# Expert weights loaded by SyncE at a row number held in a register, in place of GpSimd's gather

## The chip, the cores and the metric

The kernel runs on one core of a Trainium2 chip. The metric is the device time of one execution in microseconds (us). TensorE is PE in the rows (its weight loads PEld), VectorE is DVE, ScalarE ACT, GpSimd POOL and SyncE SP; a name with a q behind it (SPq) is that engine's instruction queue, where transfers are issued.

## What is computed

The block takes x of 4 x 2048 tokens with 256 features. It normalises each token, runs attention of 16 heads with a distance bias over it, and multiplies the result by a gate that comes from a mixture of experts (8 experts with 128 hidden features, two chosen for a token, and a shared one). The experts are what the change touches.

```python
xn = layernorm(x)
s = attention(xn)                       # 4 batches x 16 heads, 2048 keys, bias -slope*|i-j|
topk_idx = top_k(masked, 2)[1]          # two experts of 8 for a token
comb = (one_hot(topk_idx, 8) * topk_w[..., None]).sum(1)
g = einsum('th,ehi->tei', xn, w_gate)
u = einsum('th,ehi->tei', xn, w_up)
y = einsum('tei,eih->teh', silu(g) * u, w_down)
routed = einsum('teh,te->th', y, comb)
shared = silu(xn @ sw_gate) * (xn @ sw_up) @ sw_down
return x + s * silu(routed + shared)
```

## The kernel before

The program has three stages that follow one another. `tokens_stage` normalises, projects to queries, keys and values, and writes packed expert weights to a scratch tensor `w_rows` in DRAM: 8 experts x 128 rows, each row 768 floats (gate and up weights of one input row as pairs of half-precision numbers, then the row of the down weights). `attend_stage` does the attention and, spread through it, the routing and the experts. `deliver_stage` projects the heads' results, multiplies by the gate and stores.

In `attend_stage` the scores of all 64 heads (4 batches x 16) are cut into 1306 chunks of at most 1024 columns. Every engine runs the same list of chunks in its own written order: PE computes the scores of chunk c+3 (`scores`, L1385), ACT takes the exponential of chunk c (L1502), DVE multiplies the diagonal pieces (`fade`, L1527), and PE multiplies the probabilities with the values (`weighted_sum`, L1411). The heads alternate between wide ones (up to 32 chunks) and narrow ones (down to 8).

The experts' work is hung into this list. Routing sorts all token choices by expert into 72 tiles of 256 slots. `owner` (128 x 72 whole numbers, written by DVE in L1714) holds, for tile i and partition p, the row of `w_rows` that partition p needs: 128 times the tile's expert, plus p. `row_of` holds the tokens of a tile, `back_of` the places for its results. Once DVE has written these (`order_ready`, L1576, at chunk 209 in head 10), tile i goes through these steps, each fixed to a chunk by the table `FF_AT`, one tile for each 11300 columns (`FF_EACH`): PE turns the token rows (`turn_tile`, L1441), DVE takes them (L1550, L1552), PE multiplies with gate and up weights (`gate_up`, L1451, after a wait for `w_in`), ACT and DVE form the hidden features (L1493, L1583, L1586), PE multiplies with the down weights (`down`, L1457, which raises `ff_down`), DVE copies the result (L1593).

The weights of three tiles have room at a time (`w[:, i % 3, :]`), the token rows (`xs`) and results (`ys`) of two. GpSimd does all the traffic by indirect transfers, in a written order with waits for a chunk number (`expd`), the pace: for tile i two stores of the results of tile i-1 (`store_rows`, L1334), two gathers of the token rows of tile i+2 (`load_rows`, L1328), one gather of the weights of tile i+2 (`load_weights`, L1322). The pace numbers are columns behind the turn of a tile: stores at 500 and 5100, token rows at 2800 and 7400, weights at 9700.

SyncE runs a loop over the 64 heads n. In it, in this order: it waits until the result of head n-1 has been read out (`out_ready`) and stores it (`store_head`, L987 and L988); in some heads it loads the sums of a batch; it loads the raw values of head n+2 (`load_v`, L1079); it waits until all scores of head n are done (`scored`) and loads keys and queries of head n+3 (`load_head`, L1071, four transfers of 256 KB). DVE turns the keys of head n+3 (`turn_k`, L1514) in the middle of head n+2.

Of the kernel before, what the change touches and what calls it, by code (L numbers as in the profile page):

```python
# [19 lines left out]
P = 128  # L20
# [21 lines left out]
SLOTS = 3  # L42
# [13 lines left out]
MIX_FROM, MIX_TO = 364, 397  # L56
PAIRS_AHEAD = 2
PADDING = P
PACE_YS, PACE_XS, PACE_W = (500, 5100), (2800, 7400), 9700
BIAS = 1 + 3 * HD  # L60
STEEP = 3
XS = 2.0 ** 11
# [1003 lines left out]
def load_head(engine, keep, n):  # L1066
    par = n % STACKS
    for dst, stack in ((keep["K"][par], keep["k_stack"]), (keep["Q"][par], keep["q_stack"])):
        rows = stack[row_of_head(n) * HALF:(row_of_head(n) + 1) * HALF, :]
        for half in range(2):  # L1070
            engine.dma_start(dst[HALF * half:HALF * (half + 1), :], rows).then_inc(keep["stacks_in"][par], 16)  # L1071


def load_v(engine, keep, n):
    par = n % 2
    b, h = divmod(row_of_head(n), H)
    v_rows = keep["values"].rearrange("(j p q) k -> j p (q k)", p=P, q=TT)
    src = v_rows[b * BPB:(b + 1) * BPB, :, h * TT * HD:(h + 1) * TT * HD].rearrange("g p k -> p g k")
    engine.dma_start(keep["V_raw"][par][:].rearrange("p (g t) d -> p g (t d)", g=BPB), src).then_inc(keep["v_loaded"][par], 16)  # L1079


def attend_stage(nc, a, keep):
# [54 lines left out]
    with ExitStack() as ctx:  # L1137
# [106 lines left out]
        with nc.Block() as block:  # L1244
            @block.sync
            def _(sp):
                def load_sums(b):
                    for par in range(2):
                        sp.wait_ge(o_out[par], STORED * (H // 2) * (b + 1))
                    if b > 0:  # L1250
                        sp.wait_ge(inverted, 6 * b)
                        sp.wait_ge(proved, 9 * b)
                    sp.dma_start(sums[:], keep["sums"][(b + 1) * H:(b + 2) * H, :].rearrange("h (e c) -> (h e) c", c=D)).then_inc(sums_in, 16)
                    load_shifts(sp, keep, b, sums_in)

                def store_recips(b):
                    sp.wait_ge(inverted, 6 * (b + 1))
                    store_inverse(sp, keep, b, recip_out)

                load_head(sp, keep, 2)  # L1260
                for dst, src in route_loads:
                    sp.dma_start(dst, src).then_inc(route_loaded, 16)

                sp.dma_start(keep["stats"], keep["stat"][0:3 * VW].rearrange("p j t -> p (j t)")).then_inc(peaks_out, 16)

                def load_pair():
                    sp.wait_ge(peaks_out, 16)
                    sp.wait_ge(routed, 1)
                    for b in range(B):
                        sp.dma_start(q_peaks[:, b], keep["stats"][0:H, b * KT:(b + 1) * KT].rearrange("h (e t) -> h e t", t=2)).then_inc(peaks_in, 16)  # L1270
                    sp.dma_start(keep["limit"][:], a["limit"]).then_inc(peaks_in, 16)
                    sp.dma_start(k_peaks.rearrange("p b k -> p (b k)"),
                                 keep["stats"][VW:VW + H, :].unsqueeze(1).broadcast_to([H, P // H, B * KT])).then_inc(peaks_in, 16)

                for n in range(BH):
                    b, h = divmod(n, H)
                    if n >= 1:
                        sp.wait_ge(out_ready, n)
                        store_head(sp, keep, n - 1, o_out)
                    if b > 0 and h == 2:  # L1280
                        load_sums(b - 1)
                    if b > 0 and h == SIDE_FROM + 1:
                        store_recips(b - 1)
                    if n + STACKS == H:
                        sp.wait_ge(const_in, 48 * (B - 1))
                    if n == H + 1:
                        load_pair()
                    if n + 2 < BH:

                        sp.wait_ge(v_in, n + 1)  # L1290
                        load_v(sp, keep, n + 2)
                    if n + STACKS < BH:
                        sp.wait_ge(scored, FIRST_CHUNK[n + 1])
                        load_head(sp, keep, n + STACKS)
                    if b == 0 and 3 <= h < 3 + 3 * (B - 1):
                        store_constant(sp, a, keep, (h - 3) // 3 + 1, (h - 3) % 3, const_in)
                sp.wait_ge(recip_out, 48 * (B - 1))
                sp.wait_ge(scored, FIRST_CHUNK[BH - 1])
                for n in range(2):
                    sp.dma_start(keep["inverse"][0:3 * H, n, :], keep["turned"][3 * H * n:3 * H * (n + 1), :]).then_inc(keep["inverse_in"][n], 16)  # L1300
                sp.dma_start(keep["spread"][:].bitcast(U16).rearrange("k c p -> k (c p)"), a["spread"]).then_inc(keep["w_o_in"], 16)
                sp.dma_start(keep["w_o"][:], a["wT_out"].rearrange("(c p) n -> p c n", p=P)).then_inc(keep["w_o_in"], 16)
                sp.dma_start(keep["b_o"], a["b_out"].rearrange("(o n) -> o n", o=1).broadcast_to([P, D])).then_inc(keep["w_o_in"], 16)
                with nc.allow_non_contiguous_dma(reason="256 biases, once"):
                    sp.dma_start(keep["b_v"], a["b_qkv"].rearrange("(c p) -> p c", p=P)[:, 2 * DC:3 * DC]).then_inc(keep["w_o_in"], 16)
                sp.wait_ge(mixed, NT)
                for u in range(BPB):
                    load_block(sp, a, keep, u, keep["o"][:, u], keep["x"][:, u], keep["block_in"][u])

                sp.wait_ge(o_out[0], STORED * (BH // 2))  # L1310
                sp.wait_ge(o_out[1], STORED * (BH // 2 - 1))

            @block.gpsimd
            def _(pool):
                index = lambda ap: bass.IndirectOffsetOnAxis(ap=ap, axis=0)

                def load_weights(i):
                    if i > 2:
                        pool.wait_ge(ff_down, i - 2)
                    if i > 1:  # L1320
                        pool.wait_ge(expd, after("turn", i - 2, PACE_W))
                    nc.gpsimd.indirect_dma_start(w[:, i % 3, :], None, keep["w_rows"], index(keep["owner"][:, i:i + 1])).then_inc(w_in[i % 3], 16)  # L1322

                def load_rows(i, t):
                    if i > 1:
                        pool.wait_ge(ff_turned, i - 1)
                        pool.wait_ge(expd, after("turn", i - 2, PACE_XS[t]))
                    nc.gpsimd.indirect_dma_start(xs[:, i % 2, t, :], None, keep["xn"], index(row_of[:, t, i:i + 1])).then_inc(xs_in[i % 2], 16)  # L1328

                def store_rows(i, t):  # L1330
                    pool.wait_ge(ff_y, i + 1)
                    if i + 1 < TILES_IN:
                        pool.wait_ge(expd, after("turn", i + 1, PACE_YS[t]))
                    nc.gpsimd.indirect_dma_start(keep["ys"], index(back_of[:, t, i:i + 1]), ys[:, i % 2, t, :], None).then_inc(ys_out[i % 2], 16)  # L1334

                def fetch(j):

                    if j >= PAIRS_AHEAD:
                        pool.wait_ge(mixed, TT * (j - PAIRS_AHEAD + 1))
                    for n in range(2):  # L1340
                        pool.wait_ge(expd, fetch_at(j, n))
                        pool.dma_start(pairs[:, j % PAIRS_AHEAD, n], returned[n, j]).then_inc(mix_in[j % PAIRS_AHEAD], 16)

                pool.wait_ge(routed, 1)
                pool.wait_ge(order_ready, 1)
                for i in range(2):
                    load_weights(i)
                    for t in range(2):
                        load_rows(i, t)
                for i in range(TILES_IN):  # L1350
                    for t in range(2):
                        if i > 0:
                            store_rows(i - 1, t)
                        if i + 2 < TILES_IN:
                            load_rows(i + 2, t)
                    if i + 2 < TILES_IN:
                        load_weights(i + 2)
                for t in range(2):
                    store_rows(TILES_IN - 1, t)
                for n in range(2):  # L1360
                    pool.wait_ge(ys_out[n], 32 * (TILES_IN // 2))
                for j in range(NBLK):
                    fetch(j)
# [1837 lines left out]
```

## Time and profile before

| what | value |
|---|---|
| median of three runs | 1667.21 us |
| lowest and highest of them | 1664.34 and 1673.85 us |
| the profiled execution, its own time | 1676.03 us |
| its span, first to last instruction | 1674.1 us |
| mean granted TensorE clock in it | 0.976 |
| PE busy over the span | 1524.8 us (91%) |
| ACT busy | 1318.0 us (79%) |
| DVE busy | 1010.6 us (60%) |
| POOL busy | 496.4 us (30%) |

The busy shares are means over three unlike stages. `attend_stage` lies from about 277 to 1580 us of the span, and the experts' tiles in it from about 484 to 1455 us. The profile's chain of work that ended last reaches back only to about 1581 us, into `deliver_stage`, so it says nothing of the stretch that the change touches; that stretch is read from its windows, its waits and its order of time.

### The profile page before, as it was taken

The page shows a single profiled execution, that of the slowest core. Times are in us where ns is not written, and L with a number is a line of the kernel's source. Part 1 is how long each engine was busy: PE and PEld are TensorE (multiplying, and loading weights), DVE is VectorE, ACT ScalarE, POOL GpSimd, SP SyncE. Part 2 cuts the span into 40 slices and gives each one's busy share as a digit, 9 for nine tenths or more (in the row PEclk, how much of TensorE's full clock was granted, in tenths as well). Part 3 has the DMA queues.
Part 4 walks back from the last instruction along what each step waited for, and adds up shares of the span by engine and source line. Part 5 has one row for each costly group of instructions (what it writes and reads, how often), then busy time and mean ns, then how long its engine had stood idle before and what let it go on. Part 6 is the DMA issues. An engine that isn't in the chain of part 4 may idle for free. (4 is left out here: it accounts for less than half of the span.)

```text
span 1674.1 us, 39958 instructions
## 1 busy us (share of the span) xinstructions
PE 1524.8 (91%) x15328; PEld 680.6 (41%) x15328; DVE 1010.6 (60%) x2738; ACT 1318.0 (79%) x1694; POOL 496.4 (30%) x477
## 2 busy tenths in 40 slices
PE   5898997899989999998999899989999899988996
PEld 3554564223334443343444333434443333322464
DVE  7787765988854454545445444454455444577776
ACT  5788776888888887887888788878888788788721
POOL 1222331000023343343343343434333333222053
PEclk9999998999999999999999999999999999999999
DMA  6858776233345455454444455544545554577795
GB/s 202 274 193 253 259 228 183 68 112 90 90 143 132 131 138 141 138 137 128 137 134 134 126 139 137 140 132 134 131 134 143 135 134 134 132 203 221 244 313 173
DMA packets 201089, 265.58 MB, mean 159 GB/s; under 512 B 90960, under 2 KB 158592, under 8 KB 200640
## 3 DMA queue, kind: packets, MB, share of 16 engines
q1 hardware_dynamic: 168256, 171.72, 36.8%
q0 software_dynamic: 24192, 82.86, 16.1%
q10 hardware_dynamic: 8448, 8.39, 1.4%
q8 instruction: 125, 2.05, 0.5%
q14 instruction: 68, 0.56, 0.1%
HBM read 180.56 MB, written 90.46 MB: 162 GB/s over the span
## 5 line engine op out<-in xcount | busy, mean ns | idle before, releaser
L1502 ACT ACTIVATE probs_att<-SC_att 128x1024 f32<-128x1024 f32 (+10 forms) x1306 | 1075.2, 911 | 181.5 <-PE SC_att L1385 160.4
L1411 PE MATMUL O_att<-probs_att,V_att 128*32 128x512 f32 (+7 forms) x8144 | 642.5, 412 | 50.3 <-DVE probs_att L1527 28.4
L1527 DVE TENSOR_TENSOR probs_att<-probs_att,decay 128x128 f32<-128x128 f32 x1024 | 264.3, 286 | 272.6 <-ACT probs_att L1502 245.9
L1411 PEld LDWEIGHTS O_att<-probs_att,V_att 128*32 128x32 f32 x8144 | 178.4, 111 | 208.7 <-issue 129.4
L1385 PE MATMUL SC_att<-Q,K_turned_att 64*128 64x512 f16 (+7 forms) x1244 | 221.6, 310 | 13.9 <-issue 5.6
L1334 POOL DMA_INDIRECT ys<-ys_att,back_of_att x144 | 144.7, 1005 | 252.9 <-ACT probs_att L1502 226.8
L1328 POOL DMA_INDIRECT x<-xn,row_of_att x144 | 142.8, 992 | 243.2 <-ACT probs_att L1502 226.3
L1385 PE MATMUL SC_att<-Q,K 64*128 64x512 f16 (+9 forms) x1154 | 201.2, 301 | 7.6 <-DVE K_turned_att L1514 7.0
L1385 PEld LDWEIGHTS SC_att<-Q,K_turned_att 64*128 64x128 f16 x1244 | 67.2, 94 | 265.2 <-ACT probs_att L1502 156.7
L1322 POOL DMA_INDIRECT x<-w_rows,owner x72 | 71.9, 999 | 333.6 <-DVE row_of_att L1576 217.3
L699 POOL TENSOR_TENSOR inverse<-qk_tok,inverse 128x512 f16<-128x512 f32 x64 | 75.6, 1189 | 171.4 <-ACT inverse L731 164.3
L1451 PE MATMUL F_att<-x 128*128 128x256 f16 x864 | 111.6, 281 | 1.5 <-issue 1.3
L1385 PE MATMUL SC_att<-inverse,K_turned_att 64*128 64x512 f16 (+7 forms) x602 | 106.3, 309 | 6.2 <-issue 4.5
L1533 DVE COPY out<-O_att 128x512 f32<-128x512 f32 x64 | 44.2, 691 | 105.5 <-PE O_att L1411 89.6
L599 PE MATMUL GU_tok<-xT_tok,w_qkv_tok 128*128 128x512 f16 x384 | 90.9, 388 | 15.5 <-DVE xT_tok L916 15.4
L1385 PEld LDWEIGHTS SC_att<-Q,K 64*128 64x128 f16 (+1 forms) x1154 | 65.4, 95 | 96.8 <-ACT probs_att L1502 46.9
L1457 PE MATMUL F_att<-x 128*128 128x256 f32 x288 | 82.9, 411 | 18.3 <-DVE x L1586 16.3
L1385 PE MATMUL SC_att<-inverse 64*128 64x512 f16 (+8 forms) x560 | 96.7, 299 | 0.4 <-ACT probs_att L1502 0.4
L1593 DVE COPY ys_att<-F_att 128x512 f32<-128x512 f32 x72 | 49.8, 691 | 77.6 <-PE F_att L1457 71.8
L1451 PEld LDWEIGHTS F_att<-x 128*128 128x128 f16 x864 | 80.9, 100 | 26.8 <-issue 15.9
L1550 DVE TENSOR_SCALAR x<-F_att 128x512 f16<-128x512 f32 x72 | 49.7, 690 | 61.5 <-PE F_att L1441 48.2
L1385 PEld LDWEIGHTS SC_att<-inverse,K_turned_att 64*128 64x128 f16 x602 | 32.6, 94 | 122.8 <-ACT probs_att L1502 65.5
(212 smaller groups left out, 1672.4 us busy)
## 6 DMA issues: line engine op xcount, KB each, us to landing
K<-k_stack SPq DMA_DIRECT2D x86, 256.0 KB
Q<-q_stack SPq DMA_DIRECT2D x86, 256.0 KB
x<-ys POOLq DMA_DIRECT2D x32, 512.0 KB, 4.8
x<-in_x SPq DMA_DIRECT2D x24, 512.0 KB, 6.7
k_stack<-inverse SPq DMA_DIRECT2D x96, 128.0 KB
q_stack<-inverse SPq DMA_DIRECT2D x96, 128.0 KB
inverse<-k_stack SPq DMA_DIRECT2D x42, 256.0 KB
inverse<-q_stack SPq DMA_DIRECT2D x42, 256.0 KB
```

Source lines behind the costliest of these rows:

```text
L599: mm = pe.matmul(GU[:, m, :], w_qkv[:, w, c, m * P:(m + 1) * P], xT[:, j % 2, x, c, :], start=(k == 0), stop=(k == len(PRODUCTS) - 1))
L699: nc.gpsimd.tensor_tensor(parts[:, k, 1, :], qk[:, m, :], parts[:, k, 0, :], ALU.subtract).then_inc(part2, 1)
L1322: nc.gpsimd.indirect_dma_start(w[:, i % 3, :], None, keep["w_rows"], index(keep["owner"][:, i:i + 1])).then_inc(w_in[i % 3], 16)
L1328: nc.gpsimd.indirect_dma_start(xs[:, i % 2, t, :], None, keep["xn"], index(row_of[:, t, i:i + 1])).then_inc(xs_in[i % 2], 16)
L1334: nc.gpsimd.indirect_dma_start(keep["ys"], index(back_of[:, t, i:i + 1]), ys[:, i % 2, t, :], None).then_inc(ys_out[i % 2], 16)
L1385: mm = pe.matmul(SC[:, c % SLOTS, at:at + x1 - x0], (K_turned[at_turned] if side else K[at_k])[rows, k * P:(k + 1) * P], Q[at_k][rows, x0: ...
L1411: mm = pe.matmul(O[VW * g:VW * (g + 1), col:col + width * len(mine)], V[par][:, k, :], spans[:, j0:j0 + BPB * (len(mine) - 1) + 1:BPB, :], ...
L1451: mm = pe.matmul(F[:, n * TILE_IN:(n + 1) * TILE_IN], w_of(i, wp, c, n), xT[:, xp, c, :], start=(k == 0), stop=(k == len(PRODUCTS) - 1))
L1457: mm = pe.matmul(F[:, t * D:(t + 1) * D], hid[:, t * P:(t + 1) * P], w[:, i % 3, WGU:WROW], start=True, stop=True)
L1502: nc.scalar.activation(probs[home][:, side + chunk.base:side + chunk.base + chunk.width], SC[:, c % SLOTS, start:start + chunk.width], ACT ...
L1527: v.tensor_tensor(diag, diag, decay[:, head_of(chunk.head), :], ALU.mult).then_inc(faded, 1)
L1593: v.tensor_copy(ys[:, i % 2].rearrange("p t d -> p (t d)"), F[:]).then_inc(ff_y, 1)
```

## The change

`load_weights` moves from GpSimd's program to SyncE's. There it waits for the buffer (`ff_down`), reads the first row number of the tile from `owner` into a register (`value_load`), and issues one plain transfer of 128 rows of `w_rows` from that row on. The first three tiles' weights are loaded in the loop's round for head 11, behind `load_v`; those of a later tile i in the round of the head in which tile i-3 is done with its down product, also behind `load_v` and ahead of the wait and the loads of `load_head`. GpSimd's five transfers of a tile become four, and their pace numbers change: stores at 500 and 6100, token rows at 3300 and 8900.

```diff
-PACE_YS, PACE_XS, PACE_W = (500, 5100), (2800, 7400), 9700
+PACE_YS, PACE_XS = (500, 6100), (3300, 8900)
@@ block.sync
+                def load_weights(i):
+                    if i > 2:
+                        sp.wait_ge(ff_down, i - 2)
+                    first = sp.value_load(keep["owner"][0:1, i:i + 1], min_val=0, max_val=(E - 1) * P)
+                    sp.dma_start(w[:, i % 3, :], keep["w_rows"][bass.ds(first, P), :]).then_inc(w_in[i % 3], 16)
+
@@ loop over the heads, behind load_v
+                    if n == CHUNKS[ORDER_AT].head + 1:
+                        sp.wait_ge(routed, 1)
+                        sp.wait_ge(order_ready, 1)
+                        for i in range(3):
+                            load_weights(i)
+                    for i in range(3, TILES_IN):
+                        if n == max(CHUNKS[ORDER_AT].head + 1, CHUNKS[FF_AT[i - 3]["down"] + SLOTS].head):
+                            load_weights(i)
                     if n + STACKS < BH:
                         sp.wait_ge(scored, FIRST_CHUNK[n + 1])
                         load_head(sp, keep, n + STACKS)
@@ block.gpsimd
-                def load_weights(i):
-                    if i > 2:
-                        pool.wait_ge(ff_down, i - 2)
-                    if i > 1:
-                        pool.wait_ge(expd, after("turn", i - 2, PACE_W))
-                    nc.gpsimd.indirect_dma_start(w[:, i % 3, :], None, keep["w_rows"], index(keep["owner"][:, i:i + 1])).then_inc(w_in[i % 3], 16)
-
                 for i in range(2):
-                    load_weights(i)
                     for t in range(2):
                         load_rows(i, t)
...
-                    if i + 2 < TILES_IN:
-                        load_weights(i + 2)
```

## Rows read from the trace of the kernel before

**Rows 1.** The page's first part: busy time of each engine, share, instructions.

```profile
PE 1524.8 (91%) x15328; PEld 680.6 (41%) x15328; DVE 1010.6 (60%) x2738; ACT 1318.0 (79%) x1694; POOL 496.4 (30%) x477
```

**Rows 2.** Windows: the order's stretch, then all tiles; busy us, clock, DMA share.

```profile
core 0: us, PE busy (x) PEld busy (x) DVE busy (x) ACT busy (x) POOL busy (x), PEclk, DMA share, GB/s
480.00:500.00 20.00, 15.21 (x193) 6.64 (x184) 7.93 (x30) 14.17 (x19) 8.08 (x6) 0.83 0.70 218
500.00:1450.00 950.00, 900.30 (x9811) 380.15 (x9814) 467.19 (x1275) 795.88 (x1001) 348.39 (x351) 0.98 0.50 134
```

**Rows 3.** Groups by line, 500 to 1450 us: busy, mean ns, idle before, releasers.

```profile
L1411 PE MATMUL O_att<-probs_att,V_att 128*32 128x64 f32 (+7 forms) x5832 | 452.2, 408 | 22.3 <-DVE probs_att L1527 9.7 <-DVE out L1533 7.6 <-issue 4.5
...
L1451 PE MATMUL F_att<-x 128*128 128x256 f16 x864 | 111.6, 281 | 1.5 <-issue 1.3
L1457 PE MATMUL F_att<-x 128*128 128x256 f32 x284 | 81.7, 411 | 17.9 <-DVE x L1586 16.3 <-issue 1.5
...
L1322 POOL DMA_INDIRECT x<-w_rows,owner x70 | 67.6, 966 | 116.0 <-ACT probs_att L1502 81.1 <-PE F_att L1457 29.1 <-issue 5.8
```

**Rows 4.** The tile `w_rows`: GpSimd's gather, ns min/median/max, and us to landing.

```profile
L1322 POOL DMA_INDIRECT x<-w_rows,owner x72: 945/947/3332, 484.1 to 1424.0; - x72
...
DMA to landing us min/median/max: 3.0/3.8/5.9
```

**Rows 5.** SyncE in order of time, head 11: start us, us.

```profile
490.48 2.52 SPq L987 DMA_DIRECT2D weighted<-out  x4
...
493.64 0.45 SPq L1079 DMA_DIRECT2D V_raw<-values  x1
```

**Rows 6.** Line 3168, the program's one register load from on-chip memory: ns on SyncE.

```profile
L3168 SPq TENSOR_LOAD <-redo x1: 493/493/493, 1669.7 to 1669.7; - x1
...
L3168 SPq FUSED_REGOPS  x1: 192/192/192, 1670.3 to 1670.3; - x1
L3168 SPq SEQ_ASSERT  x1: 37/37/37, 1670.5 to 1670.5; - x1
```

**Rows 7.** Line 1071, the loads of a head's keys and queries: ns of an issue.

```profile
L1071 SPq DMA_DIRECT2D K<-k_stack x86: 465/594/1845, 125.1 to 1526.1; - x86
```

**Rows 8.** PE in order of time, then line 1451's own row: products with tiles' weights.

```profile
503.06 1.49 PE L1451 MATMUL F_att<-x 128*128 128x256 f16 x12
...
L1451 PE MATMUL F_att<-x x864: 269/273/421, 503.1 to 1448.1; 128*128 128x256 f16 x173
```

**Rows 9.** The tile `x` (the experts' buffers lie in it): us to landing, all transfers.

```profile
DMA to landing us min/median/max: 3.8/5.4/11.7
```

**Rows 10.** SyncE's and PE's order of time around tile 45, the shortest lead.

```profile
1073.61 0.44 SPq L1079 DMA_DIRECT2D V_raw<-values  x1
...
1097.35 1.48 PE L1451 MATMUL F_att<-x 128*128 128x256 f16 x12
```

**Rows 11.** SyncE's own waits over the whole span: us in total, times, longest.

```profile
SPq L1071 <- PE SC_att L1385: 667.9, 46, 26.2
SPq L987 <- DVE out L1533: 197.0, 61, 16.9
```

**Rows 12.** SyncE's and DVE's order of time for head 18: keys loaded, keys turned.

```profile
596.43 1.13 SPq L1071 DMA_DIRECT2D K<-k_stack  x2
...
619.99 0.75 DVE L1514 TENSOR_SCALAR K_turned_att<-K,turn 128x2048 f16<-128x2048 f16 x1
```

**Rows 13.** GpSimd's and PE's order of time for tile 63: rows gathered, rows turned.

```profile
1323.26 0.97 POOL L1328 DMA_INDIRECT x<-xn,row_of_att  x1 [6.95 <-ACT probs_att L1502]
...
1337.04 0.66 PE L1441 MATMUL F_att<-ident,x 128*128 128x128 f32 x4
```

**Rows 14.** Line 1514 on DVE, 500 to 1450 us: ns min/median/max of the keys' turns.

```profile
L1514 DVE TENSOR_SCALAR K_turned_att<-K,turn x31: 743/748/919, 501.9 to 1438.8; 128x2048 f16<-128x2048 f16 x31
L1514 DVE TENSOR_SCALAR K_turned_att<-inverse,turn x15: 744/748/960, 546.6 to 1412.1; 128x2048 f16<-128x2048 f16 x15
```

**Rows 15.** The same line in the groups by line: busy us, mean ns.

```profile
L1514 DVE TENSOR_SCALAR K_turned_att<-K,turn 128x2048 f16<-128x2048 f16 x31 | 23.4, 756 | 0.0
L1514 DVE TENSOR_SCALAR K_turned_att<-inverse,turn 128x2048 f16<-128x2048 f16 x15 | 11.8, 789 | 0.0
```

## The prediction

> **What bounds the kernel now.** I read the page's busy shares first, then windows of the stretch in which the experts' tiles run, then the groups by line in that stretch, and last the order of time around a few tiles. The shares put PE first with 91% of the span and POOL last with 30% [rows 1]. The chain that ended last lies in the final stage, so the stage of the change is read from its windows. From 500 to 1450 us PE is busy 900.3 of 950 us, ACT 795.9, DVE 467.2 and POOL 348.4 [rows 2]. PE is the bound there, and all that any change of waiting can give back is the 49.7 us in which it is idle. The groups by line say who ends that idle time: 22.3 us ahead of the value products, ended by DVE, and 17.9 us ahead of the down products, ended by DVE's hidden features [rows 3]. The products with gate and up weights, the first to need a tile's weights, stood idle 1.5 us in all for 864 matmuls, and no transfer is named [rows 3]. So the weights' arrival doesn't hold PE today. What the reader is to see: GpSimd's gather of the weights has 67.6 us of busy time, but 116.0 us of idle time ahead of it, ended by ACT and PE, which is the written pace [rows 3]. POOL waits for the others; nobody waits for POOL.
>
> **The change part by part.** *GpSimd's 72 gathers go.* 72 x 0.947 us = 68 us less for an engine that is idle 950 - 348.4 = 602 us of the stretch [rows 2, 4]. Worth nothing on PE's path; the cover is POOL's own idle time.
>
> *The bytes stay.* Each load moves 128 rows of 3072 bytes as before, on the same DMA engines, whose mean share is 0.50 [rows 2].
>
> *SyncE gets 72 loads.* The trace has no such load, so its issue is bounded. The one register load that SyncE does, at the program's end, takes 0.493 us, with 0.192 us of register work and 0.037 us of a bounds test [rows 6]; the issue of a 256 KB transfer takes 0.465 to 1.845 us, median 0.594 [rows 7]. Together 1.3 us; the address worked out from the register is not shown, one more 0.192 at the least. I take 1.5 us, with 1.2 and 3.0 as the ends (the long issue, and two more pieces of register work). 72 x 1.5 = 108 us for an engine that stands waiting 667.9 us for PE's scores and 197.0 us for DVE's read-outs [rows 11].
>
> *Landing.* The gather lands 3.0 to 5.9 us after its issue, median 3.8 [rows 4]; transfers into that buffer memory of any kind take up to 11.7 us [rows 9]. A plain load of the same bytes is nearest to the gather, so 3.8; the range goes to 11.7.
>
> *The first tile is the tight place.* Before, its gather started as soon as the order was ready. After, SyncE must first wait for the read-out of head 10, store it and load values: in the trace these issues begin at 490.48 and end at 493.64 + 0.45 = 494.09 us [rows 5]. The first load is issued by 494.09 + 1.5 = 495.6 and lands at 495.6 + 3.8 = 499.4. PE needs it at 503.06 [rows 8]: 3.7 us to spare. Cost nothing; if the cover goes, that is if landing takes over 7.5 us, PE stands still by the excess.
>
> *All later tiles.* I placed every load into the trace's times (the end of the values' load in its head, or the down product three tiles before, whichever is later, and 1.5 us for each load in turn) and took the distance to the tile's first product. The shortest from tile 2 on is tile 45: SyncE is free at 1073.61 + 0.44 = 1074.05, has issued at 1075.55, and PE needs the weights at 1097.35 [rows 10]: 21.8 us against a landing of 3.8, or 11.7 at worst. Cost nothing.
>
> *What is queued behind the new wait.* SyncE now waits for `ff_down` in the round for head n, ahead of the loads of head n+3's keys. That product stands in PE's order near the scores of head n itself, for which the key loads wait anyway, so they start later by about one load and no more: 1.5 to 2.5 us by the same placing. These keys are turned half a wide and a narrow head later; the shortest distance is head 18, keys issued at 596.43, turned by DVE at 619.99 [rows 12], 23.6 us. PE waits for the turned keys, so it would take over ten us of delay per head to matter. Cost nothing.
>
> *The later pace.* The tiles' first products run from 503.1 to 1448.1 us over 71 steps of 11300 columns [rows 8], 13.3 us a step, so the 1500 columns by which the second row gather moves are 1.8 us, and the 1000 of the second store 1.2 us. The shortest distance from a second gather's issue to the turn of its rows (leaving out tile 0, which has no pace) is tile 63: 1323.26 to 1337.04 [rows 13], 13.8 us, then 12.0, still over the 11.7 us worst case. Cost nothing.
>
> *DVE's keys.* The only instruction that shows traffic from POOL is the turn of the keys: 748 ns at the median, up to 960 [rows 14]. Summed, 23.4 + 11.8 - 46 x 0.743 = 1.0 us over 46 turns [rows 14, 15]. The weights are 70 of POOL's 351 instructions in that stretch [rows 2, 3], so a fifth of it goes: 0.2 us, on an engine that is half idle.
>
> The sum against the profiled execution: 1676.03 - 0 (gathers) + 0 (loads, waits, pace) - 0.2 = 1675.8 us, 0.01% less. That execution is 0.5% above the median of the three runs, so I put the forecast at the median, 1667 us.
>
> **The rivals.** *Faster: the gathers disturb DVE more than the means tell.* For it: the turned keys do take up to 212 ns longer [rows 14]. The Trainium skill says on its page "SBUF — State Buffer", in "Who interferes with whom", that DVE in its two-port modes and GpSimd exclude one another for a whole instruction, and on "DMA: Bandwidth & Descriptors", in "SWDGE vs HWDGE vs iDMA", that transfers issued from SyncE are free of that. By that rule every gather that meets such an operation costs the later one its wait; the trace agrees as far as that spread of 212 ns goes. Worked out: were all 46 turns hit by the full 212 ns, all by the weights, and all on PE's path, 9.8 us would come back, 1657.4 us. Against it: the mean excess is 22 ns, and the idle time ahead of the score products isn't put down to the keys. Chance 0.11, at 1657 to 1658.
>
> *Slower: the first weights are late, PE stops and its clock falls.* The place is tile 0's gate product; it decides from a landing of over 7.5 us. What speaks for it: from 480 to 500 us PE was already short of work (15.21 of 20 us), and its granted clock was 0.83 there, a third of the stretch at the lower of its two levels, 1.2 GHz, against 0.98 over the tiles [rows 2]; the DMA share there was 0.70. Three loads, 1.2 MB, are issued in a row. On "DMA: Bandwidth & Descriptors", in "Queues, rings and completion order", the Trainium skill says that each SyncE transfer is worked off in the order of its ring, where GpSimd's has a ring of its own that takes turns with it; the weights would then stand behind the head's store. No run here shows this yet. With 11.7 us [rows 9] the stall is 4.2 us, and a second stretch at 0.83 costs 0.17 x 20 = 3.4 us: 1667.2 + 7.6 = 1674.8. From 12.4 us on it is over 0.5%; at 14 us it gives 1667.2 + 6.5 + 3.4 = 1677. Against: the median of 3.8 us, and a once-only price. Chance of over 0.5%: 0.08.
>
> *Slower: loads of keys late.* If a load held SyncE by over 20 us, PE would stop once for each head. The bound of 3.0 us per load and three loads in a head give 9.0 us against 23.6. Chance 0.02, at 1680 or more.
>
> **How the numbers follow.** A measurement of this kernel can tell about 0.5%, 8.3 us, from no change; its three runs span 9.5 us. Same: 1 - 0.11 - 0.08 - 0.02 = 0.79, at 1667 us. Its own range, 1667 less and plus 8.3, is 1659 to 1675.5; it leaves out 0.21, and the unknown costs (0 to 7.6 us for the first tile) lie within it, so I take it as the range.
>
> **What would show it.** After the change POOL's busy time should fall by about 68 us with PE's busy time and PE's idle time ahead of the gate products unchanged; SyncE should show 72 register loads of about 0.5 us and its waits for PE's scores should shrink by about 108 us. The first load should be issued near 495 us and land before 503. I would be wrong if the gate products show idle time ended by a transfer, if turned keys become the end of a wait ahead of the scores, if the row gathers with the later pace hold the turns, or if PE's granted clock over the tiles differs from 0.98.

## The result: 0.6% faster, and the profile after

The changed kernel takes 1661.47 us, median of 20 runs (1654.23 to 1670.68), the kernel before 1671.72 (1661.47 to 1680.50, 20 runs): ratio 0.994, 95% interval 0.9926 to 0.9955. That is about 10 us less. The time lies in the range that was given. The prediction's likeliest case was "same", 0.5% to either side; as a ratio to the kernel before, the 0.6% measured lies a little outside of that, on the faster side, and the interval (0.45 to 0.74%) reaches inside. The profiled execution takes 1660.71 us, 15.3 us less than that of before; its granted clock is 0.986 against 0.976.

The page's busy times of the changed kernel, and the windows of the order's stretch and of all tiles, against [rows 1, 2]:

```profile
PE 1512.7 (91%) x15328; PEld 676.3 (41%) x15328; DVE 1011.4 (61%) x2738; ACT 1318.7 (80%) x1694; POOL 429.3 (26%) x405
```

```profile
480.00:500.00 20.00, 16.95 (x237) 7.43 (x230) 10.99 (x37) 17.64 (x24) 7.25 (x5) 1.00 0.79 238
500.00:1450.00 950.00, 902.06 (x9866) 379.66 (x9863) 468.70 (x1287) 805.62 (x1010) 287.21 (x286) 0.99 0.50 136
```

POOL is 67 us less busy, as forecast. The last line shows the gain: in the same 950 us PE's busy time is nearly the same (902 against 900 us), but 9866 matmuls ran in it and not 9811, and ACT did 1010 operations and not 1001. That is 0.6% more matmuls in 0.2% more busy time. Over the whole span the same 15328 matmuls are 12.1 us less of busy time (1512.7 for 1524.8 us), and PE's idle time, span less busy, falls by 3.3 us (146.0 for 149.3). The clock over the tiles is 0.99 and not 0.98.

The groups by line of the changed kernel, 500 to 1450 us (busy, mean ns, idle before and its releasers); the lines shifted by 4, so L1415 answers to L1411 of [rows 3], L1455 to L1451, and L1518 to the L1514 of [rows 15]:

```profile
L1506 ACT ACTIVATE probs_att<-SC_att 128x1024 f32<-128x1024 f32 (+8 forms) x938 | 781.9, 902 | 123.9 <-PE SC_att L1389 111.7 <-issue 6.8 <-PE O_att L1415 0.5
L1415 PE MATMUL O_att<-probs_att,V_att 128*32 128x512 f32 (+7 forms) x5868 | 454.8, 408 | 20.1 <-DVE probs_att L1531 9.8 <-issue 5.9 <-DVE out L1537 3.9
...
L1455 PE MATMUL F_att<-x 128*128 128x256 f16 x856 | 108.4, 277 | 1.0 <-issue 0.8
...
L1518 DVE TENSOR_SCALAR K_turned_att<-K,turn 128x2048 f16<-128x2048 f16 x31 | 23.6, 761 | 0.1
L1518 DVE TENSOR_SCALAR K_turned_att<-inverse,turn 128x2048 f16<-128x2048 f16 x15 | 11.3, 752 | 0.0
```

What changed is the part of the value products' idle time that DVE's read-outs (`out`) end, 7.6 to 3.9 us, and ACT's idle time ahead of the exponentials. In the kernel before that group reads:

```profile
L1502 ACT ACTIVATE probs_att<-SC_att 128x1024 f32<-128x1024 f32 (+9 forms) x929 | 771.9, 900 | 131.9 <-PE SC_att L1385 111.9 <-issue 11.6 <-remote 3.1
```

The part with a named releaser, PE's scores, is the same (111.9 and 111.7). What shrinks is "issue" and "remote". "Issue" is idle time in which the engine waited for nothing that the profile shows, "remote" a wait whose end it can put down to no instruction of this core: the profile has no work to name for either.

**One place, read closely.** Set chunk against chunk by the starts of ACT's exponentials, the distance between the two profiles changes by at most 0.01 us from one chunk to the next in 725 of the 928 chunks of the tiles. At the last chunk the changed kernel is 13.3 us ahead, most of it won in a few steps: 3.8 us from 480 to 500 us, 4.3 us from 930 to 950 and 3.7 us from 1310 to 1320. At each of these the kernel before has two to four indirect transfers that start under 1.6 us behind another, the changed kernel two at the first and none at the others. The second of them is the end of head 33. In the kernel before, POOL, ACT and PE in order of time (start us, us, idle before), and then 14 us from there as a window:

```profile
935.54 0.95 POOL L1322 DMA_INDIRECT x<-w_rows,owner  x1 [5.71 <-ACT probs_att L1502]
936.79 0.99 POOL L1334 DMA_INDIRECT ys<-ys_att,back_of_att  x1 [0.30 <-issue]
938.28 0.97 POOL L1328 DMA_INDIRECT x<-xn,row_of_att  x1 [0.49 <-issue]
...
939.87 1.94 ACT L1502 ACTIVATE probs_att<-SC_att 128x1024 f32<-128x1024 f32 x2 [1.42 <-remote]
...
940.62 1.94 PE L1411 MATMUL O_att<-probs_att,V_att 128*32 128x512 f32 x8 [2.64 <-DVE out L1533]
```

```profile
939.00:953.00 14.00, 12.38 (x75) 3.96 (x75) 4.87 (x12) 9.44 (x11) 3.16 (x4) 0.76 0.33 98
```

The same place in the changed kernel:

```profile
932.87 0.99 POOL L1341 DMA_INDIRECT ys<-ys_att,back_of_att  x1 [1.00 <-ACT probs_att L1506]
935.58 0.97 POOL L1335 DMA_INDIRECT x<-xn,row_of_att  x1 [1.73 <-ACT probs_att L1506]
...
931.07 6.70 ACT L1506 ACTIVATE probs_att<-SC_att 128x1024 f32<-128x1024 f32 x7
...
935.32 1.07 PE L1415 MATMUL O_att<-probs_att,V_att 128*32 128x512 f32 x8 [0.95 <-DVE out L1537]
```

```profile
934.00:948.00 14.00, 13.05 (x102) 4.42 (x106) 6.68 (x16) 12.91 (x15) 3.91 (x4) 1.00 0.58 157
```

Before, three indirect transfers start 1.25 and 1.49 us apart. Behind them ACT and PE both stand still (1.42 and 2.64 us), and then the same 8 matmuls take 1.94 us where they take 1.07 after. In the kernel before PE is for a part of the stretch at the lower level of its clock (0.76 granted over it, 1.00 after); an estimate of what that takes from PE, worked out from these two shares, is 0.24 x 14 = 3.4 us at most. With the gather gone, two transfers start 2.71 us apart: ACT works on without a stop (7 exponentials from 931.07 to 937.77 us), PE stands still for 0.95 us and not 2.64, and its clock stays up. The experiments test whether the transfers are the reason.

### The profile page after: what moved, and what is told of

It is laid out like the page before. It is cut to its first block and busy times, and to the rows that moved or that the text cites. A ratio compares the mean times of both kernels' runs of the same rounds, so it can differ in the third digit from the quotient of the medians.

```text
span 1658.7 us, 40250 instructions
## 1 busy us (share of the span) xinstructions
PE 1512.7 (91%) x15328; PEld 676.3 (41%) x15328; DVE 1011.4 (61%) x2738; ACT 1318.7 (80%) x1694; POOL 429.3 (26%) x405
## 5 line engine op out<-in xcount | busy, mean ns | idle before, releaser
L1415 PE MATMUL O_att<-probs_att,V_att 128*32 128x512 f32 (+7 forms) x8144 | 637.8, 410 | 49.7 <-DVE probs_att L1531 26.1
L1335 POOL DMA_INDIRECT x<-xn,row_of_att x144 | 146.8, 1019 | 546.9 <-ACT probs_att L1506 327.7
L1415 PEld LDWEIGHTS O_att<-probs_att,V_att 128*32 128x32 f32 x8144 | 177.2, 110 | 207.0 <-issue 121.8
L1455 PE MATMUL F_att<-x 128*128 128x256 f16 x864 | 109.2, 277 | 1.0 <-issue 0.8
L599 PE MATMUL GU_tok<-xT_tok,w_qkv_tok 128*128 128x512 f16 x384 | 90.6, 387 | 13.4 <-DVE xT_tok L916 13.3
L1461 PE MATMUL F_att<-x 128*128 128x256 f32 x288 | 81.9, 407 | 17.3 <-DVE x L1590 15.7
L1455 PEld LDWEIGHTS F_att<-x 128*128 128x128 f16 x864 | 79.8, 99 | 24.8 <-issue 14.9
L1554 DVE TENSOR_SCALAR x<-F_att 128x512 f16<-128x512 f32 x72 | 49.7, 690 | 60.2 <-PE F_att L1445 32.5
L1608 DVE SCALAR_TENSOR_TENSOR gate_all<-x,share,gate_all 128x256 f32<-128x256 f32 x128 | 61.4, 482 | 11.9 <-DMA x<-ys 9.6
```

The costliest lines, as they stand in the source:

```text
L599: mm = pe.matmul(GU[:, m, :], w_qkv[:, w, c, m * P:(m + 1) * P], xT[:, j % 2, x, c, :], start=(k == 0), stop=(k == len(PRODUCTS) - 1))
L1415: mm = pe.matmul(O[VW * g:VW * (g + 1), col:col + width * len(mine)], V[par][:, k, :], spans[:, j0:j0 + BPB * (len(mine) - 1) + 1:BPB, :], ...
L1455: mm = pe.matmul(F[:, n * TILE_IN:(n + 1) * TILE_IN], w_of(i, wp, c, n), xT[:, xp, c, :], start=(k == 0), stop=(k == len(PRODUCTS) - 1))
L1461: mm = pe.matmul(F[:, t * D:(t + 1) * D], hid[:, t * P:(t + 1) * P], w[:, i % 3, WGU:WROW], start=True, stop=True)
L1608: v.scalar_tensor_tensor(out=acc, in0=pairs[:, j % PAIRS_AHEAD, n, k, :], scalar=keep["share"][:, n, t:t + 1], in1=acc, op0=ALU.mult, op1= ...
```

## The experiments

The theories. G: each indirect transfer of GpSimd holds up results of PE. B: the gather's bytes in GpSimd's queue meet other loads. P: the pace makes the gain. L: luck with the clock, which leaves the ratio between 0.993 and 1.002. Each ratio is to the kernel before, run on the same chip beside it.

**e1_sp_old_pace: the move alone.** The row transfers stay where they were.

```diff
-PACE_YS, PACE_XS = (500, 6100), (3300, 8900)
+PACE_YS, PACE_XS = (500, 5100), (2800, 7400)
```

> The changed kernel with the pace numbers of the kernel before (stores at 500 and 5100, token rows at 2800 and 7400): the move of the weights alone. Theory G (each of GpSimd's indirect transfers holds up PE's results for a moment, so 72 fewer of them are the gain): ratio 0.994. Theory P (the later, wider pace is the gain): 1.000. Theory B (the gather's bytes meet the loads of a head's keys at a bad moment, SyncE puts them in order): 0.994. Theory L (only where PE's clock happens to fall, no cause in the change): anywhere from 0.993 to 1.002.

Measured: 1658.55 us, 0.9918 (0.9895 to 0.9941). The move alone makes the whole gain; P falls.

**e2_gather_new_pace: the pace alone.** The kernel before with GpSimd's gather, at the new places.

```diff
-PACE_YS, PACE_XS, PACE_W = (500, 5100), (2800, 7400), 9700
+PACE_YS, PACE_XS, PACE_W = (500, 6100), (3300, 8900), 10300
```

> The kernel before with the changed kernel's pace for stores and token rows, the weights still gathered by GpSimd, at 10300 columns between its neighbours at 8900 and 11800: the pace alone. Theory G: 1.000. Theory P: 0.994. Theory B: 0.998 to 1.000, as the gather still meets the keys' loads now and then. Theory L: anywhere from 0.993 to 1.002.

Measured: 1681.31 us, 1.0054 (1.0035 to 1.0073). The later places are a loss when a gather is kept: it now stands 1400 columns behind a row gather and not 2300, and 1500 ahead of the next store and not 2100.

**e3_sp_tiny_gathers: the instruction without the bytes.** SyncE loads the weights, and GpSimd does 72 indirect transfers of 16 bytes a row into a spare tile at the gathers' old places. The line that issues one (the waits ahead of it are those of the gather):

```diff
...
+nc.gpsimd.indirect_dma_start(idle[:], None, few, index(keep["owner"][:, i:i + 1])).then_inc(idle_in, 16)
...
```

> SyncE loads the weights as in the changed kernel, but GpSimd keeps an indirect transfer at each of the 72 old places, with the old pace and the same 128 row numbers, of 16 bytes a row into a tile that nobody reads. The number of GpSimd's transfers is that of the kernel before, their bytes are those of the changed kernel. Theory G: the gain is lost, ratio 1.000 (0.998 to 1.002) and 0.006 over the move alone. Theory B: the gain stays, 0.994. Theory P: 1.000, and no different from the move alone with the old pace. Theory L: anywhere from 0.993 to 1.002.

Measured: 1665.99 us, 0.9961 (0.9948 to 0.9974). 7.4 us more than e1: an indirect transfer that moves next to nothing gives back half of the gain. The other half, 0.26 to 0.52% of the time of the kernel before, stays.

**e4_no_weights: the bytes away.**

```diff
-                    if i + 2 < TILES_IN:
+                    if i + 2 < 3:
...
-                        pe.wait_ge(w_in[i % 3], 16 * (i // 3 + 1))
+                        pe.wait_ge(w_in[i % 3], 16)
```

> The kernel before without the weights' transfers of tiles 3 to 71 (left out: those tiles compute with the weights of tiles 0 to 2), old pace: 69 of GpSimd's transfers and their bytes are gone and nothing takes their place. Theory G: 0.994, the same as the move alone. Theory B: 0.994 or a little less, 0.992, since the bytes are gone too. Theory P: 1.000. If it is well below the move alone, SyncE's loads cost something of their own.

Measured: 1661.71 us, 0.9935 (0.9913 to 0.9958). Leaving the weights' transfers out gains no more than loading them by SyncE does: so the bytes of a plain load cost nothing that shows.

**e5_sp_tiny_16: fewer row numbers.** As e3, with 16 rows a transfer.

> The kernel with SyncE's loads and 72 tiny GpSimd transfers, but each fetches 16 rows of 16 bytes where it fetched 128. If a GpSimd transfer costs by the row numbers it works through, an eighth of the 7.4 us is left: 0.9 us over the version without tiny transfers, ratio about 0.992. If it costs by the instruction, nothing changes: about 0.996. If clock luck made the difference between those two versions, anything from 0.990 to 0.998.

Measured: 1669.64 us, 0.9982 (0.9965 to 1.0000). No cheaper than 128 rows: the price is the instruction's, not the row numbers'. By this run 0.0 to 0.35% is left to the kernel before, by e3 more (0.26 to 0.52%): whether the bytes of an indirect transfer have a share is not settled by these two.

**e6_sp_tiny_two: twice as many.** As e3, and for 70 of the tiles a second tiny one at 3950 columns, between the row transfers at 2800 and 5100.

> SyncE's loads and two tiny GpSimd transfers for each tile, the second about halfway between two row gathers, where GpSimd is idle. If each transfer costs about 0.10 us wherever it lies: 144 x 0.10 = 14.8 us over the version without, ratio about 1.000. If only transfers that follow one another at once cost (three in a row at a tile's end), the second is free: 0.996, as with one.

Measured: 1703.75 us, 1.0181 (1.0156 to 1.0206). Both expectations are wrong by far: by the two ratios the 70 more cost 37 us where the first 72 cost 7. So the price depends on the place, and the linear form of G falls. So does L, whose range ends at 1.002.

**e7_pool_plain: the same engine, another form.** GpSimd keeps the weights, at the old places, by a plain transfer.

```diff
-nc.gpsimd.indirect_dma_start(w[:, i % 3, :], None, keep["w_rows"], index(keep["owner"][:, i:i + 1])) ...
+first = pool.value_load(keep["owner"][0:1, i:i + 1], min_val=0, max_val=(E - 1) * P)
+pool.dma_start(w[:, i % 3, :], keep["w_rows"][bass.ds(first, P), :]) ...
```

> The kernel before, but GpSimd loads each tile's weights with a plain transfer at a row number read into a register, at the old places and the old pace: the same queue, the same bytes, no list of row numbers. If the list is what costs (an indirect transfer): about 0.992, as with SyncE. If GpSimd's queue costs, whatever the form: 1.000. If half is the list and half the bytes in that queue: 0.996.

Measured: 1659.31 us, 0.9905 (0.9885 to 0.9924). The whole gain, without SyncE. The line of its weights, and GpSimd's DMA queue (packets, MB, share) in this run and then in the kernel before:

```profile
L1323 POOL DMA_DIRECT2D x<-w_rows x72: 567/580/1035, 487.0 to 1413.2; - x72
```

```profile
q0 software_dynamic: 24192, 82.86, 16.5%
```

```profile
q0 software_dynamic: 24192, 82.86, 16.1%
```

580 ns at the median where the gather took 947 [rows 4], in the same queue, with the same packets and bytes. B falls: it is neither the engine nor the queue but the indirect form. The Trainium skill says on "DMA: Bandwidth & Descriptors", in "Issuing engines are not separate DMA queues", that starting transfers from several engines saves only the time that it takes to issue them; e7 against e1 agrees (0.9905 and 0.9918), for plain transfers.

**e8_early: the price in an empty stretch.** 135 tiny transfers at chunks 20 to 154, where the kernel before has POOL idle: 45 indirect ones of 128 rows, 45 of 16 rows, 45 plain ones.

> SyncE's loads at the old pace, and in the attention of the early heads, where GpSimd is idle in the kernel before, 135 tiny GpSimd transfers, one at each of chunks 20 to 154: 45 indirect ones of 128 rows, 45 indirect ones of 16 rows, 45 plain ones of 128 rows, all 16 bytes a row. Read by the times of ACT's exponentials against those of the kernel before, with the 45 chunks after them as control. If a transfer costs 0.10 us there too: 4.6 us more over the first 45 chunks; over the second 0.6 us if the rows cost, 4.6 if the instruction does; over the third 4.6 if the queue costs and 0 if the list does. If a transfer disturbs only a stretch that PE bounds with tiles' work beside: 0 everywhere.

Four windows of 45 chunks each, from chunk 20 on (bounds: the starts of ACT's exponentials), in the kernel before and then in this one:

```profile
295.12:338.76 43.64, 35.92 (x409) 10.29 (x411) 41.19 (x104) 38.59 (x47) 0.00 (x0) 1.00 0.26 62
338.76:382.13 43.37, 39.54 (x426) 12.47 (x418) 37.62 (x155) 37.23 (x46) 0.00 (x0) 0.96 0.38 108
382.13:425.96 43.83, 41.12 (x434) 13.85 (x430) 38.80 (x177) 39.53 (x46) 0.00 (x0) 1.00 0.32 86
425.96:469.25 43.29, 40.30 (x432) 13.62 (x433) 38.03 (x174) 38.21 (x47) 0.00 (x0) 1.00 0.33 87
```

```profile
290.28:363.88 73.60, 44.48 (x407) 12.97 (x411) 43.49 (x109) 40.05 (x46) 47.43 (x45) 0.80 0.27 38
363.88:439.81 75.93, 53.10 (x433) 15.21 (x425) 37.89 (x153) 38.50 (x46) 40.10 (x46) 0.79 0.23 62
439.81:484.30 44.49, 41.62 (x423) 13.51 (x423) 37.96 (x172) 39.64 (x47) 23.62 (x44) 0.96 0.38 87
484.30:527.58 43.28, 40.30 (x432) 13.62 (x433) 38.02 (x174) 38.22 (x46) 1.01 (x2) 1.00 0.33 87
```

The same 45 chunks take 73.60 us for 43.64 beside 45 indirect transfers of 128 rows, 75.93 for 43.37 beside those of 16 rows, and 44.49 for 43.83 beside 45 plain ones; the control agrees to 0.01 us. That is about 0.7 us for each indirect transfer in such a series, one to a chunk, and 0.015 for a plain one. The clock is lower there, too: 0.80 and 0.79 are granted in the first two windows, where the kernel before has 1.00 and 0.96. How much of the 0.7 us that makes isn't measured. In order of time, within the first group:

```profile
349.56 1.34 POOL L1365 DMA_INDIRECT idle_att<-w_rows,idx_att  x1 [0.31 <-issue]
350.04 0.39 PE L1409 MATMUL SC_att<-Q,K 64*128 64x512 f16 x2
351.19 0.95 POOL L1365 DMA_INDIRECT idle_att<-w_rows,idx_att  x1 [0.30 <-issue]
351.70 1.94 ACT L1526 ACTIVATE probs_att<-SC_att 128x1024 f32<-128x1024 f32 x2 [2.63 <-PE SC_att L1409]
352.78 0.39 PE L1409 MATMUL SC_att<-Q,K_turned_att 64*128 64x512 f16 x2 [2.35 <-issue]
```

PE's scores end at 350.43, and ACT, which waits for nothing else, starts on them at 351.70: the result was 1.27 us late. The next products of PE wait 2.35 us for "issue".

**How late results are, counted.** For each of PE's results over the tiles (500 to 1450 us) I took the time from the end of its last matmul to the record of its semaphore, and summed those over 0.3 us ("held"). Beside it stands how often an indirect transfer started under 1.6 us behind the one before it ("close"). Both are worked out from the semaphore and instruction records of one profile per kernel. Where indirect transfers run, some of the semaphore records are missing (in the kernel before there are 1413 for 1526 such results of PE; in e12 1555 for 1555), so the sums are rough: by the way in which records are matched to results, that of the kernel before comes out between 76 and 107 us and that of e11 between 115 and 269. That of e12 is zero either way. The bound of 1.6 us was chosen with all runs in hand; the expectations of e11 and e12, which follow below, rest on the held results of the runs ahead of them.

```
kernel                             close   held us   ratio
e12 no indirect transfer at all        0       0.0   0.9871
changed kernel (and again as e9)       3      40.2   0.9940 (0.9960)
e10, e1 SyncE's loads, old pace     5, 7  45.1, 43.0 0.9916, 0.9918
e4  no weights                         9      36.3   0.9935
e7  plain weights on GpSimd           11      40.9   0.9905
e5  SyncE + 72 tiny, 16 rows          37      87.1   0.9982
before                                41      84.7   1
e3  SyncE + 72 tiny                   42      91.8   0.9961
e2  gather, new pace                  58     118.0   1.0054
e6  SyncE + 142 tiny                 150     244.6   1.0181
e11 SyncE, rows close                150     207.7   1.0249
```

On the whole the ratio follows the close pairs. From e10 to the kernel before, 36 more pairs cost 13.1 us, 0.36 us each; to e11, 145 more cost 54.5 us, 0.38 each; by the ratios e6 gives 0.31, e5 0.34, e2 0.43, e3 0.20. Two runs don't fit: the changed kernel has the fewest pairs of those with indirect transfers and isn't the fastest, and e3 has 42 pairs and is 0.4% faster than the kernel before with 41. In the kernel before, 25 of the 41 pairs are a weights gather with the next store close behind it. Beyond the bound the spacing seems to cost little: e10 has 72 transfers that start under 2.0 us behind another, the changed kernel 48, and e10 is the faster.

There is a reading that needs no semaphore record. Where ACT stood ready before its scores were done, it began within 0.08 us of their last matmul's end in all 275 cases of e12. In the kernel before it began over 0.3 us late in 22 of 250 cases, 15.7 us in all and up to 2.34 us, in the changed kernel in 12 of 275, 7.4 us in all. DVE, where it stood idle ahead of a diagonal piece, began within 0.10 us of the end of ACT's exponential in all 230 cases of the kernel before. So what comes late is what PE hands on to ACT, not what ACT hands on to DVE.

**e11_close: only the spacing.** SyncE's loads, the same four indirect row transfers, 1300 columns apart; the edit against e10:

```diff
-PACE_YS, PACE_XS = (500, 5100), (2800, 7400)
+PACE_YS, PACE_XS = (500, 3100), (1800, 4400)
```

> SyncE's loads, the same four indirect row transfers for each tile, but 1300 columns apart (about 1.5 us) where they were 2300 (2.7 us). If an indirect transfer holds PE's results up at a price that doesn't depend on its neighbours: 0.992, nothing changed. If one that follows another closely costs most (with a second tiny transfer, those 1150 columns behind another held PE's results up by 1.2 to 1.3 us on the mean, those 2300 behind by 0.2): three of four now follow closely, 216 against 144 there for 45 us, so some 60 us more, ratio about 1.03.

Measured: 1711.75 us, 1.0249 (1.0215 to 1.0282). Nothing added and nothing moved but the spacing, and the kernel is 54.5 us slower than e10. The rule of the close pairs forecast it. The rows' bytes move closer together here too; e6 has as many close pairs with transfers that move next to nothing and loses 0.31 us a pair to e11's 0.38. Plain row transfers at this spacing were not run.

**e12_plain_rows: no indirect transfer.** The places are those of e10.

```diff
-nc.gpsimd.indirect_dma_start(xs[:, i % 2, t, :], None, keep["xn"], index(row_of[:, t, i:i + 1])) ...
+pool.dma_start(xs[:, i % 2, t, :], keep["xn"][(2 * i + t) % NROWS * P:((2 * i + t) % NROWS + 1) * P, :]) ...
```

(the stores likewise)

> SyncE's loads, and GpSimd's row transfers as plain ones of fixed rows, at the same places and of the same bytes. This leaves out the routing of rows to experts: each tile takes a fixed block of rows and stores to a fixed place. If indirect transfers hold PE's results up and plain ones don't: the 288 that are left go too, and the 43 us of held results over the tiles with them; by the rate so far (72 gathers: 44 us of held results, 14 us of time) another 12 to 16 us, ratio about 0.983. If the row transfers are spaced well enough to cost nothing: 0.992.

Measured: 1650.02 us, 0.9871 (0.9839 to 0.9903); 7.2 us less than e10, where 12 to 16 were expected. The groups over the tiles:

```profile
L1508 ACT ACTIVATE probs_att<-SC_att 128x1024 f32<-128x1024 f32 (+9 forms) x948 | 789.1, 905 | 116.1 <-PE SC_att L1391 111.0
L1417 PE MATMUL O_att<-probs_att,V_att 128*32 128x512 f32 (+6 forms) x5916 | 462.1, 411 | 15.1 <-DVE probs_att L1533 9.8 <-issue 4.5 <-DVE out L1539 0.3
```

ACT's idle time ended by "issue" and "remote" is gone from the row, and the 7.6 us of the value products ended by `out` are 0.3. No result is late by over 0.3 us, out of 1555. So held results come with the indirect form, and spaced ones still cost a little; how much is less sure, since e12 also moves rows that lie together where the routed ones lie scattered.

**e9_after and e10_old_pace: the pace once more, side by side.**

> The changed kernel itself, its four row transfers of a tile evenly spaced (2800 columns apart). It was 0.994 of the kernel before. If the later pace is worth nothing either way, it equals the next run, 0.992 to 0.994 both; if it costs about 3 us, the next run is lower by 0.002.

> SyncE's loads with the row transfers at the places of the kernel before (2300 columns apart, then a gap). First measured at 0.9918. If that was luck it comes back to 0.994, the changed kernel's ratio; if the old places are better, again about 0.992.

Measured: 1663.47 us, 0.9960 (0.9942 to 0.9977), and 1657.24 us, 0.9916 (0.9888 to 0.9944). The old places are better by 6 us here and 3 the first time, though both kernels have few close pairs (3 and 5) and held results alike. The mean granted clock of the runs is 0.982 and 0.986. Why the even spacing loses that isn't settled. SyncE's loads with the old pace (e1, e10) beat both kernels given.

## Why the range held and the mechanism did not

*The range.* It held in part by luck. The sum was 0.2 us less than before; the runs show about 10 us less. The forecast stood at 1667 us, the median of three runs, and the 20 runs of the kernel before have theirs at 1671.72. From there the same 8.3 us to either side would begin at 1663.4 us, above the 1661.47 measured.

*The bound.* PE, right. But "all that any change of waiting can give back is the 49.7 us in which it is idle" counts the wrong time. PE's idle time over the tiles went only from 49.7 to 47.9 us, and most of the gain is busy time: 12.1 of 15.4 us over the two spans, for the same matmuls. A wait that ends with PE at the lower level of its clock comes back as longer matmuls (1.94 for 1.07 us at head 33), and these count as busy. An unchanged busy time of PE was a sign that the prediction named, and it did not hold.

*GpSimd's gathers go: the step that failed.* "Worth nothing on PE's path; the cover is POOL's own idle time." POOL's 602 idle us are real and hide POOL's own work; they don't hide what an indirect transfer does to PE. The term was set to 0 and is 13 to 14 us with the pace kept (e1 14.4 us, e10 13.1 us). There was a sign of it in [rows 3]: the 22.3 us ahead of the value products were read as DVE's, but their 7.6 us ended by `out` go almost wholly when no transfer is indirect (0.3 in e12). Much of it was PE's own results coming late to DVE.

*The bytes stay.* Right for plain loads: e4 and e7.

*SyncE's 72 loads.* Taken at 1.5 us each. In the changed kernel, the register load by its line (ns min/median/max, first and last start), then the tile `w_rows` with the issue and the us to landing:

```profile
L1263 SPq TENSOR_LOAD <-owner x72: 265/428/658, 492.4 to 1399.7; - x72
L1263 SPq FUSED_REGOPS  x72: 152/159/184, 492.9 to 1400.1; - x72
```

```profile
L1264 SPq DMA_DIRECT2D x<-w_rows x72: 13/347/381, 493.4 to 1400.5; - x72
...
DMA to landing us min/median/max: 3.3/4.0/5.9
```

0.428 + 0.159 + 0.347 and some 0.1 of small pieces make 1.0 us, below the lower end of 1.2; landing 4.0 for 3.8. SyncE's waits, against [rows 11]:

```profile
SPq L1263 <- PE F_att L1461: 356.6, 47, 12.2
SPq L1071 <- PE SC_att L1389: 246.9, 48, 21.7
SPq L987 <- DVE out L1537: 163.8, 55, 16.9
```

Most of the wait for the scores became a wait for `ff_down` (356.6 us), a wait for work that SyncE would have waited for anyway: the three add up to 767 us for 865, 98 less. The forecast was 108 less ahead of the scores alone; there it is 421 less, since the new wait took its place.

*The first tile.* SyncE, then PE:

```profile
493.42 2.64 SPq L1264 DMA_DIRECT2D x<-w_rows  x3
...
498.89 1.38 PE L1455 MATMUL F_att<-x 128*128 128x256 f16 x11
```

No stall and no transfer is named ahead of the gate products (1.0 us of idle time in 856 matmuls). The clock from 480 to 500 us is 1.00 and not 0.83, and 3.8 us of the gain lie in this stretch, so the rival of the late first weights went the other way.

*Keys.* Head 18: loaded at 592.15, turned at 616.03, 23.9 us for the 23.6 of [rows 12]. Right.

*The later pace, "cost nothing".* Not borne out: e9 against e10 puts it at 6 us, the changed kernel against e1 at 3, and e2 at 8 with the gather kept and moved too.

*DVE's keys, and the faster rival.* The turns sum to 23.6 + 11.3 us for 23.4 + 11.8 [rows 15]: 0.3 us. The time came out on the faster side, but not by GpSimd and DVE excluding one another. The Trainium skill's page "SBUF — State Buffer" says in "Who interferes with whom": "PE and ACT never wait on anyone." It speaks of ports of the on-chip memory, which no run here tests. It can't be carried over to time: results of PE were 1.27 us late beside indirect transfers (e8) and none was over 0.3 us late beside plain ones (e12).

*What was listed as a sign of error.* The granted clock over the tiles did differ, 0.99 for 0.98. It is a part of the price: at head 33 PE's stop comes first and the lower level after it. How the 0.36 us of a pair divide between the two isn't measured.

## What to carry to other kernels

Where the rows to be fetched are contiguous, a plain transfer at a row number in a register replaces an indirect one, on GpSimd as well as on SyncE, and it is worth it even where GpSimd is idle two thirds of the time. Indirect transfers that must stay should be kept apart: here each that started under 1.6 us behind another cost 0.2 to 0.4 us of the kernel's time, and places 2300 columns apart, about 2.7 us, did best. Wider even spacing did no better (e9 against e10), so it is worth trying more than one. Idle time ended by "issue" or "remote", and a step that returns only at some places of two otherwise equal profiles, is worth following to what another engine did there, even one that nobody waits for.

## What was not expected of the hardware

Results of PE come late beside indirect transfers of GpSimd, whether these move 128 rows or 16 (e8: 45 chunks take 73.60 and 75.93 us for 43.64 and 43.37), and worst when the transfers follow one another closely (e11: 54.5 us slower than e10 by the spacing alone). Beside plain transfers of the same engine no result of PE was over 0.3 us late (e12), and plain loads of the weights in the same queue gave the whole gain (e7). ACT's results show nothing of the kind: in the kernel before DVE began within 0.10 us of the end of an exponential in all 230 cases in which it had stood idle ahead of a diagonal piece. The semaphore records themselves say less of this, for near indirect transfers many are missing (ACT has 855 for 1000 results over the tiles in the kernel before, 1019 for 1019 in e12). What links GpSimd's indirect transfers to PE's results isn't visible in these traces and stays open.
